# Last layer of a four-layer kernel: three batches in work, `x` added to the mixed terms on POOL, loras in 64-row pairs, centring inside the pick matrices

## What is computed

```
lora(z, n) = ll_n + tanh(z @ la_n.T) @ lb_n.T
dx    = shift(x) - x                  # the token before, zero for the first
lerpx = x + dx * xw
n     = (x + dx * lora(lerpx, n)) @ nW.T                 for n in r, k, v, g
w     = exp(-exp(lora(x + dx * lora(lerpx, d), d)))
# 16 heads of 8 channels, state of 8 x 8 each, over the 512 tokens:
kv    = k_t (outer) v_t
y     = r_t . (state + u * kv)
state = w_t * state + kv
o     = silu(g) * layernorm_of_each_head(y) * ln_w + ln_b ; out = o @ oW.T
ffn   = gelu(xn @ W1t.T + b1) @ W2t.T + b2               # W1t, W2t: ternary weights
x     = x + out + ffn
```

## Time and profile before

| | us |
|---|---|
| median of 3 runs (1919.16 to 1919.61) | 1919.44 |
| the profiled execution | 1919.56 |
| its span in the profile | 1917.8 |
| the last layer in it, from its first instruction (1557.5) to the output transfer's issue (1911.1) | 353.6 |

### The profile page before, as it was taken

One profiled execution on the slowest core, in us unless ns is written; L12 is line 12 of the kernel. 1 busy time (PEld: TensorE's weight loads), 2 busy tenths in 40 slices (PEclk: granted clock), 3 DMA queues, 4 the chain that ended last, 5 costly groups with the idle time before them and its releaser, 6 DMA issues. The chain is left out here.

```text
span 1917.8 us, 23240 instructions
## 1 busy us (share of the span) xinstructions
PE 1765.0 (92%) x8678; PEld 1032.3 (54%) x8678; DVE 1014.4 (53%) x1676; ACT 845.4 (44%) x1025; POOL 329.3 (17%) x274
## 2 busy tenths in 40 slices
PE   6599999998887998999999999999999978999995
PEld 4222222222553445787878787878787824444442
DVE  3454545444675444544545454545445456777665
ACT  4467777785433333343434333333434243434341
POOL 1000000000463002112121212020303022232222
PEclk8689999998777999999999999999999989999998
DMA  1222222122002640000000000000000010000001
GB/s 72 41 51 45 45 45 45 45 45 115 1 1 71 157 126 1 1 1 1 1 2 1 1 1 1 1 1 1 1 1 1 1 52 1 0 0 0 0 0 44
DMA packets 19120, 48.95 MB, mean 26 GB/s; under 512 B 784, under 2 KB 1680, under 8 KB 18128
## 3 DMA queue, kind: packets, MB, share of 16 engines
q1 hardware_dynamic: 19024, 47.63, 10.2%
HBM read 45.14 MB, written 2.36 MB: 25 GB/s over the span
## 5 line engine op out<-in xcount | busy, mean ns | idle before, releaser
L494 ACT ACTIVATE probs<-ps_ring 128x1024 f32<-128x1024 f32 x256 | 246.1, 1024 | 126.6 <-PE ps_ring L708 123.9
L1765 PEld LDWEIGHTS ps_o<-v,probs 128*128 128x128 f32 x2048 | 235.3, 192 | 31.0 <-issue 25.6
L1765 PE MATMUL ps_o<-v,probs 128*128 128x129 f32 x2048 | 248.1, 278 | 1.7 <-ACT probs L1490 1.2
L1490 ACT ACTIVATE probs<-ps_ring 128x1024 f32<-128x1024 f32 x128 | 126.9, 1024 | 212.4 <-PE ps_ring L1746 212.3
L722 PE MATMUL ps_o<-probs,v 128*32 128x512 f32 x1024 | 140.1, 621 | 13.1 <-DVE o_sb L545 13.1
L1571 DVE TENSOR_REDUCE negmax<-ps_o 128x2 f32<-128x1024 f32 x64 | 78.5, 1226 | 137.2 <-PE ps_o L1721 137.2
L1958 POOL TENSOR_TENSOR rs<-r,state 128x512 f32<-128x512 f32 x64 | 81.6, 1275 | 206.3 <-DVE state L2050 202.6
L1483 ACT ACTIVATE xn<-ps_ring,pack 128x512 f32<-128x512 f32 x64 | 40.5, 685 | 162.6 <-PE ps_ring L1330 162.6
L708 PEld LDWEIGHTS ps_ring<-q_stack,k_stack 32*128 32x128 f32 x512 | 31.9, 188 | 123.2 <-issue 103.0
L1584 DVE RECIPROCAL rden<-ps_o 128x2 f32<-128x2 f32 x128 | 21.5, 168 | 144.1 <-PE ps_o L1765 144.1
L2050 DVE TENSOR_TENSOR_SCAN state<-decay,state,kv 128x511 f32<-128x511 f32 x64 | 91.5, 1430 | 5.9
(11 more groups left out here) (371 smaller groups left out, 3473.6 us busy)
## 6 DMA issues: line engine op xcount, KB each, us to landing
cwb<-combine_by_expert SPq DMA_DIRECT2D x8, 2048.0 KB
score<-score_by_expert SPq DMA_DIRECT2D x7, 2048.0 KB, 13.8
pack<-pack_dram SPq DMA_DIRECT2D x1, 3840.0 KB, 15.8
pack<-pack_dram SPq DMA_DIRECT2D x1, 2443.0 KB, 8.6
x<-x_in SPq DMA_DIRECT2D x2, 1024.0 KB, 6.8
out<-x SPq DMA_DIRECT2D x1, 2048.0 KB, 6.3
score<-score_by_expert SPq DMA_DIRECT2D x1, 1536.0 KB, 13.3
pack<-pack_dram SPq DMA_DIRECT2D x1, 1451.0 KB, 7.1
```

The lines of the kernel that those rows point to most:

```text
L494: nc.scalar.activation(probs[n % 3][:, 2 * half:2 * half + 2, :], ps, ACT.Exp, scale=float(HD0) ** -0.5).then_inc(read, 1)
L1490: nc.scalar.activation(probs[:, n % 2, m, :, :], ps, ACT.Exp).then_inc(read, 1)
L1765: last = nc.tensor.matmul(ps_o[:, i, k * (D + 1):(k + 1) * (D + 1)], probs[:, (b * PAIRS + p) % 2, m, j, queries], v[:, m, h, :], start=(m ...
```

## The change

All of it is in `layer3_mix` and in its constants.

- *Three batches.* A turn holds batch a at the preparation, b at the recurrence, and c = b - 1 at variance, `o`, out and the addition to x. There are ten turns, (0,-,-), (1,0,-), (2,1,0) to (7,6,5), (-,7,6), (-,-,7), all written out; r, k, decay, gate and the two halves of xv get two buffers each. The order of the ring's uses (`ring_order3`) and of all five engines' work is new.
- *x on POOL.* `mix` writes `mixed`; POOL adds `xn` to it for d, r, k and g (`add_x`). `la_dd`, r, k and g are one product each. `dx` of batch a + 1 (`step_back`) is POOL's last work of a turn.
- *Pairs.* `lb_r` and `lb_k`, and `lb_v` and `lb_g`, are products over rows 0 to 63 and 64 to 127 of the same tanh tile, one straight after the other, into two banks.
- *Centring.* `pick_j` has each head's mean taken out, and v times u's term goes through `centre_head` into `ps_y` as a product, so `ps_y` holds the centred y. ACT copies it (`yc`) and squares it.
- *Tables.* One table set is asked for by name ahead of Ln and Exp.
- *First part.* `interpolate` (the `lerp`) comes ahead of the magnitudes and the splitting of the v weights; `bounds` and DVE's ternary weight come behind `finish_v`, and POOL's ternary weight waits for the bounds and stands ahead of `dx` of batch 1.

```diff
-    pick = np.zeros((P, 8, P), np.float32)
-    for j in range(8):
-        pick[i, j, (i // 8) * 8 + j] = 1
+    same_head = i[:, None] // 8 == i[None, :] // 8
+    c["centre_head"] = np.eye(P, dtype=np.float32) - same_head.astype(np.float32) / 8
+    pick = np.stack([same_head * ((i[None, :] % 8 == j) - 1 / 8) for j in range(8)], 1).astype(np.float32)
...
+def turns3():
+
+    for t in range(-1, B + 1):
+        yield (t + 1 if t + 1 < B else None), (t if 0 <= t < B else None), (t - 1 if t >= 1 else None)
+def ring_order3():
+
+    order = []
+    for a, b, c in turns3():
+        at_turn = [("v_0", b), ("v_1", b), ("la_rk", a), ("la_vg", a), ("la_d", a), ("u", b), ("var", c), ("v_2", b), ("lb_d", a),
+                   ("v_3", b), ("lb_r", a), ("lb_k", a), ("v_4", b), ("la_dd", a), ("v_5", b), ("lb_v", a), ("lb_g", a),
+                   ("v_6", b), ("lb_dd", a), ("v_7", b), ("r", a), ("k", a), ("g", a), ("v", a)]
+        order += [use for use in at_turn if use[1] is not None]
+    return order
...
         @block.gpsimd
...
+            def add_x(a, n, name):
+                pool.wait_ge(mix_ready, 5 * a + n + 1)
+                nc.gpsimd.tensor_tensor(mixed[name][:, :], mixed[name][:, :], xn[:, at(a)], ALU.add).then_inc(mixed_ready, 1)
...
+            for a, b, c in turns3():
+                if b is not None:
+                    for j in range(3):
+                        times_r(b, j)
                 if a is not None:
+                    add_x(a, 0, "d")
+                if b is not None:
+                    times_r(b, 3)
+                if a is not None:
+                    add_x(a, 1, "r")
+                    add_x(a, 2, "k")
+                if b is not None:
+                    times_r(b, 4)
+                    times_r(b, 5)
+                if a is not None:
+                    add_x(a, 4, "g")
+                if b is not None:
+                    times_r(b, 6)
+                    times_r(b, 7)
+                if a == 0:
+                    pool.wait_ge(scale_step, BOUND)
                     pool.drain()
+                    ternary_weight(nc.gpsimd, pool, 1)
+                    pool.drain()
+                if a is not None and a + 1 < B:
+                    step_back(a + 1)
...
         @block.scalar
...
+            def rms(c):
+                nc.scalar.preload_act_table_set("natural_log_exp_and_others")
...
+            def take_y(b):
+                act.wait_ge(picked, (b + 1) * HD3)
+                if b:
+                    act.wait_ge(o_ready, b)
+                nc.scalar.activation(yc[:, :], ps_y[:, :], ACT.Copy)
+                nc.scalar.activation(sq[:, :], ps_y[:, :], ACT.Square).then_inc(squared, 1)
...
         @block.vector
...
+            for a, b, c in turns3():
+                if a is not None:
+                    interpolate(a)
+                if a == 0:
+                    magnitude(0)
+                    magnitude(1)
+                    nc.vector.tensor_copy(single(vw_high[:, :]), vw).then_inc(vw_high_ready, 1)
+                    nc.vector.tensor_copy(st[:, :, 0:1], w["state"].unsqueeze(2))
                 if b is not None:
+                    weigh_rk(b)
+                    scan(b, 0)
+                    scan(b, 1)
+                    weigh_v(b)
+                    scan(b, 2)
                 if a is not None:
+                    mix(a, "d")
+                if c is not None:
+                    gated(c)
+                if b is not None:
+                    scan(b, 3)
                 if a is not None:
+                    mix(a, "r")
+                    mix(a, "k")
                 if b is not None:
+                    scan(b, 4)
+                if c is not None:
+                    add_out(c)
+                if b is not None:
+                    scan(b, 5)
                 if a is not None:
+                    mix(a, "v")
+                    mix(a, "g")
+                    finish_v(a)
                 if b is not None:
+                    scan(b, 6)
+                    scan(b, 7)
+                if a == 0:
+                    bounds()
+                    ternary_weight(nc.vector, dve, 0)
+                if a is not None:
+                    take_gate(a)
 
         @block.tensor
...
+            def pair(a, low, high, of):
+                was_read(pe, ("la_" + of, a))
+                for name, rows in ((low, slice(0, 64)), (high, slice(64, P))):
+                    multiply(("lb_" + name, a), (w[f"lb_{name}"][rows, :], th[of][rows, :]))
...
+            def centred_vu(b):
+                pe.wait_ge(vu_ready, b + 1)
+                if b:
+                    pe.wait_ge(squared, b)
+                nc.tensor.matmul(ps_y[:, :], w["centre_head"], vu[:, :], start=True, stop=False)
```

More of the change, by code:

```diff
@@ L1819, in _ @@
             turn_attention(B - 1)
[L1825 to L1847, removed]
-FF_WEIGHTS = ("W1_3", "W2_3")
+FF_WEIGHTS = ("W1_3", "W2_3")
+RING3 = 4
+def turns3():
[9 more added lines that the diff above has]
+    return order
 def layer3_mix(nc, sh):
@@ L1988, in turn_program @@
                 if b is not None:
-                    gelu(0)
-                    gelu(1)
+                    for t in range(FT):
+                        gelu(b, t)
                 if a is not None:
-                    tanh("la_dd", th["dd"])
-                    src = filled(act, turn, "lb_dd")
-                    nc.scalar.activation(ew[:, :], src, ACT.Exp, bias=w["ll_d"]).then_inc(read("lb_dd"), 1)
+                    tanh(a, "dd")
+                    decays(a)
+                    take_rk(a, "r", r)
@@ L2012, in turn_program @@
[L2012 to L2021 removed]
+                    take_v(a)
@@ new lines, in multiply, with value @@
+            def multiply(use, *terms):
+                ps, done = empty(pe, use)
+                for n, (lhsT, rhs) in enumerate(terms):
+                    last = nc.tensor.matmul(ps, lhsT, rhs, start=(n == 0), stop=(n == len(terms) - 1))
+                last.then_inc(done, 1)
+            def value(name, b, part):
+                ps, done = empty(pe, (name, b))
+                cols = slice(part * P, (part + 1) * P)
+                split_products(nc, ps, (vw_high[:, cols], vw_low[:, cols]), (xv_high[:, b % 2, :], xv_low[:, b % 2, :])).then_inc(done, 1)
@@ L2207, in turn_program @@
[L2207 to L2220 removed]
+                        multiply((f"la_{n}", a), (w[f"la_{n}"], lerp[:, :]))
@@ L2236, in turn_program @@
                 if a is not None:
-                    written("lb_g")
-                    product("g", ("gW", xn[:, at(a)]), ("gW", dmix["g"][:, :]))
-                down(2)
-                down(3)
+                    pe.wait_ge(mixed_ready, 4 * a + 1)
+                    multiply(("la_dd", a), (w["la_d"], mixed["d"][:, :]))
+                if b is not None:
+                    scan_input(b, 5)
+                    pick(b, 2)
+                if c is not None:
+                    project_out(c)
@@ new lines, in _ @@
+                if a is not None:
+                    pair(a, "v", "g", "vg")
+                if b is not None:
+                    scan_input(b, 6)
+                    pick(b, 3)
+                if a is not None:
+                    was_read(pe, ("la_dd", a))
+                    multiply(("lb_dd", a), (w["lb_d"], th["dd"][:, :]))
+                if b is not None:
+                    scan_input(b, 7)
+                    pick(b, 4)
+                if a is not None:
+                    for n, name in enumerate("rk"):
+                        pe.wait_ge(mixed_ready, 4 * a + 2 + n)
+                        multiply((name, a), (w[f"{name}W"], mixed[name][:, :]))
```

488 lines of the change are left out of this document (222 added, 266 removed).

## The result

The changed kernel takes 1887.3 us (median of 4 runs, 1885.34 to 1894.49) against 1919.3 for the kernel before beside it: a ratio of 0.9846, interval 0.9824 to 0.9867. The forecast was 1873.6 in a range of 1860 to 1896. The time became shorter, as forecast, and lies in the range; the gain is 32 us instead of 46. The profiled execution took 1888.65 us, span 1886.9.

What follows compares the result with a forecast made beforehand. PE bounds middle turns; after the change a four-engine chain gives 35.0 us a turn. First part -1.7, turn 0 -8.9, six middle turns -32.3, last turn -3.0: -45.9, span 1917.8 to 1871.9, hence 1873.6 us, range 1860 to 1896.

Steps and rivals of the forecast that it cites:

- the count of its products: PE's work in a middle turn before the change: 37 f32 products at 0.86 plus 9 value products at 0.70, 38.1 us.
- T: Start of value product v_0 in a turn, the zero from which the prediction timed one middle turn.
- T of turn 0: Start of the turn that starts batch 1: equivalent to 1586.0, 1.7 us earlier than before.
- rival D: Every added POOL operation stops VectorE for its whole 1.28 us: a turn 37.0, +12, 1886 in all; chance 0.14.
- the walk: One middle turn followed through the engines from the start of v_0: 35.0 us a turn, 5.4 less than before.
- a chain through four engines: Middle turn: out, add_out to scan7, times_r(7), pick7 is late by one us against PE's own 33.3.
- The list of gaps that would prove the forecast wrong: PE gaps in a turn at la (dx late), v_7 (mix v late) or centre (weigh_v late), each put under 0.5.
- The clock: Slower PE clock at the ends: la priced at 4.4 us in the first part, 1.0 us added in the last turn.
- Refilling: 0.5 us added to each middle turn, as the turn of before also has.
- rival B: Meetings with POOL cost little and PE alone bounds: 33.3 + 0.5 = 33.8 us a turn, 1866 in all; chance 0.20.
- the prediction's upper bound for a pair: Nothing gained by the lb pairs: 1.72 us plus 0.2 for changing the tile shape twice; the forecast took 1.06.
- rival C: Halves of a pair don't overlap: +7.8, 1881, chance 0.10; or overlap in one record of two: 1877.5, chance 0.07.

Runs made afterwards that it cites:

- e12: Changed kernel with scan 6 ahead of finish_v, x through PE again and lb products full width instead of pairs: 1893.67 us, middle turn 38.0.
- e1: Changed kernel with VectorE taking scan 6 ahead of finish_v, nothing else moved: 1867.44 us, middle turn 33.9.
- e6: Changed kernel with down 0, down 1 and pick 5 ahead of product k on PE: 1870.34 us, middle turn 34.4.
- e13: Changed kernel with scan 6 ahead of finish_v, POOL's dx ahead of its ternary, pick 4 ahead of v_7, value v ahead of the last pick: 1861.86 us.
- The square: Four runs with scan 6 first. Without pairs: x on PE 1893.67 us (e12), on POOL 1873.60 (e8). With pairs: 1887.15 (e9), 1867.44 (e1).
- e9: e1 with x through PE again for la_dd, r, k and g: 1887.15 us, middle turn 37.1.
- e2: Changed kernel without pairs, the lb products over all 128 rows one after another: 1886.79 us, middle turn 36.5.
- e5: Changed kernel with two PE products that nobody reads put between r and k: 1884.85 us, middle turn 36.1.
- e8: e1 without pairs, the lb products over all 128 rows: 1873.60 us, middle turn 34.5.
- e4: Changed kernel with POOL's addition of x for g moved behind times_r(6): 1883.72 us, middle turn 36.3.

## Why the prediction was right and wrong

**Right.** The first product comes 2.5 us behind the layer's start (forecast 2.7), the gap behind POOL's ternary is 8.2. A turn without waits is the count of its products (38.1 counted, 38.0 in e12). x on POOL is worth 3.4, ScalarE has three table loads and 15.0 us a turn, and VectorE meets POOL in pieces. VectorE waits for `out` at `add_out` for 0.94 in the changed kernel, takes it up at T+19.4 (forecast T+19.2), and the last scan of the turn ends at T+31.25 (forecast T+31.5).

**Near, but by luck.** T of turn 0 was forecast at 1586.0 and came at 1586.2, because the layer began 2.2 us early; counted from the layer's start the first part is 2.4 longer than forecast, 1.9 of it up to the start of POOL's ternary (19.6 us behind the layer's start, forecast 17.7). Turn 0 is 1.3 longer, the same ring wait (1.24), and the last turn 1.3 shorter. The 1887 measured lies at rival D's 1886, but not by D's mechanism: VectorE is busy 29.06 a turn with POOL's four additions and 27.61 without them (e12), so they cost it 1.45 us and not 4 x 1.28, and in e1 PE, not VectorE, is the bound beside the same additions.

**The step that failed** is the walk: "hence a chain through four engines, out, add_out to scan7, times_r(7), pick7, is late by one us against PE's own 33.3". It followed each engine's work to the next and checked PE against the data of its products, but not against the bank each product goes into. By the walk's own times `kv` of scan 6 ends near T+27.6 and PE wants `k` near T+24.9 (measured T+27.45 and T+25.5); setting these beside each other would have shown a wait of over 2 us. The list of gaps that would prove the forecast wrong (la, `v_7`, centre) left `k` out for the same reason. In the changed kernel this wait (2.1) comes ahead of the forecast's chain and hides it. With it gone (e6) the chain gives 34.4, and its late point is pick 6, not pick 7.

**The clock** was in the prediction for the ends (0.79 and 0.90 stretches) and not for the middle, because no gap was expected there. It is 1.8 of the 3.9 us that e1 gives back each turn.

**Sizes.** Refilling: the forecast adds 0.5 us a turn for it, in its 35.0 and in rival B's 33.8. No run of the new order shows it: e12 has 37.97, less than its products' 38.1, and e6's chain gives 34.4 where the walk has 34.5. That e1 and e13 lie at B's 33.8 (33.9, 33.85) is luck in part, since other terms fill the place of the 0.5. The first is a short ring wait or load wait of about 0.2. The second is the pairs. Timeline of PE in the changed kernel, starts of a product, the pair, a value product and the next product:

```profile
1713.42 1.02 PE L2223 MATMUL ps_x<-o,pack 128*128 128x512 f32 x2
...
1714.38 1.13 PE L2182 MATMUL ps_ring<-tanh_vg,pack 64*128 64x512 f32 x4
...
1715.44 0.50 PE L1330 MATMUL ps_ring<-xv_high,vw_low 128*128 128x512 f32 x1
...
1716.25 1.02 PE L2206 MATMUL ps_y<-rs,pack 128*128 128x512 f32 x2
```

From the pair to the next product is 1.06, the forecast's figure. But the product ahead of it has 0.96 to the pair's start instead of 0.86, and the value product behind it 0.81 instead of 0.70: where the tile shape changes, 0.1 is lost on each side. This 0.2 stood in the prediction's upper bound for a pair and not in its 1.06. A pair is 1.27 all told, two of them 0.4 more per turn than I counted. The count itself, 29 x 0.86 + 2 x 1.06 + 9 x 0.70, is 33.36 where the prediction wrote 33.3; with the 0.4 it is 33.8, and e13 without its 0.16 is 33.7. The square agrees: e12 to e9 saves 0.86 a turn, 2 x (1.72 - 1.27) is 0.9.

**What stays open.** Why the last middle turn of the changed kernel kept its clock at 1.00 behind a gap as long as that of the other turns, and why the tail is slow in e2, e5 and e8 and not in the other kernels. Neither was tried.

## What to carry to other kernels

When the order of a ring's uses changes, walk the ring as well as the data: for each product, write the time at which the reader of the use four before it ends, beside the time PE wants the bank. A step that only shortens PE's work ahead of such a wait (x on POOL, pairs) buys little or nothing until the wait is gone (the pairs made the gap 0.4 longer and the turn of the trace 1.3 longer, with PE's clock). A read that frees a bank belongs ahead of operations whose result is wanted later, and useful work can fill the wait (e6).

## What the runs showed of the hardware that I had not expected

**A short gap of PE can cost almost twice its length.** In the changed kernel a gap of 2.11 to 2.13 us is followed by a stretch at the lower clock in five middle turns of six. `k` itself takes 1.10, 1.26, 1.50, 1.68 and 2.00 in them, so the clock falls at another point of the work each time, and the price is 1.8 us in each. The last middle turn has 2.13 and keeps 1.00. Turn 0 with 1.24, and in their middle turns e2 with 1.73, e4 with 1.01 and e5 with 0.41 keep 1.00 as well. In the last turn the gap ahead of `centre_head` is 2.2 in the changed kernel and in e2, e5 and e8, and only in the latter three the clock behind it is lower (0.66, 0.57 and 0.57 over some 4 us). So the gap's length isn't all that decides.

**POOL is made to wait as well,** when it comes second. The prediction had rows only for VectorE's side. Changed kernel, a middle turn:

```profile
1704.53 1.12 DVE L2105 TENSOR_TENSOR o<-yc,rstd 128x512 f32<-128x512 f32 x1
1705.06 1.72 POOL L1935 TENSOR_TENSOR mixed_d<-mixed_d,xn 128x512 f32<-128x512 f32 x1
...
1705.73 1.33 DVE L2107 TENSOR_SCALAR o<-o,pack 128x512 f32<-128x512 f32 x1
...
1712.26 1.28 DVE L2091 TENSOR_TENSOR_SCAN state<-decay,state,kv 128x511 f32<-128x511 f32 x1
...
1712.35 2.25 POOL L1935 TENSOR_TENSOR mixed_k<-mixed_k,xn 128x512 f32<-128x512 f32 x1
```

POOL's addition takes 1.27 alone. Started 0.09 into a scan it takes 2.25 while the scan keeps its 1.28; started into `o` it takes 1.72. VectorE's `tensor_scalar` then takes 1.33 instead of the 0.55 it has in the tail. The Trainium skill ("SBUF — State Buffer", who interferes with whom) has this as an exclusive lock, whichever comes first keeping it for the whole instruction. The trace agrees in both directions to some 0.2 us: a scan of 1.28 with POOL's 1.27 behind it would end 2.46 after POOL's start, and 2.25 was measured.

**The halves of a pair run interleaved.** The four records of a pair of two-record products take 1.06 us and not four times 0.43. Two of them begin at 1714.38 and two at 1714.91:

```profile
1714.38 0.70 PE L2182 MATMUL ps_ring<-tanh_vg,pack 64*128 64x512 f32 x2
...
1714.91 0.60 PE L2182 MATMUL ps_ring<-tanh_vg,pack 64*128 64x512 f32 x2
```

The trace doesn't say which record is which half's; that one of each starts together is inferred, since the two records of one product otherwise start 0.43 apart. Then the high half's first record does not stand behind the low half's second. The Trainium skill ("TensorE: Matmul & The Clock Gate", part 3) has matmuls start and end strictly in program order; by that, taken record by record, a pair would be three records and the switch, the 1.5 of rival C. The measurement decides against it for this case.
